# A vision layer on one core: the first picture pair in two parts ahead of the weights, its steps in another order, and the last four steps as straight code

## What is computed

```python
gray = einsum('bchw,c->bhw', x, (0.2989, 0.587, 0.114))
h = abs(conv3x3(gray, scharr)).sum(over the 2 filters) / 2
n = layernorm(h);  prev = n shifted by one row
k, v, r = (n * m_i + prev * (1 - m_i)) @ W_i.T       # m_i, W_i for i in k, v, r
wkv = recurrence over the rows (w, u, k, v)           # numerator / denominator
h = h + (sigmoid(r) * wkv) @ Wo.T
n2 = layernorm(h);  e = argmax(h_hat @ Wg.T)          # one expert for each row
h = h + gelu((n2 * scale_e + bias_e) @ W1_e + b1_e) @ W2_e + b2_e
```

## Time and profile before

| | us |
|---|---|
| median of 3 runs | 1120.14 (1119.8 to 1122.0) |
| the profiled execution | 1121.44 |
| its span, first to last instruction | 1119.8 |
| TensorE busy in the span | 1069.8 (96%) |
| VectorE busy | 1024.5 (91%) |
| ScalarE busy | 989.4 (88%) |

### The profile page before, as it was taken

The page is one execution under the profiler, slowest core; times in us unless marked ns, Lnnn a source line. Parts: engine busy times, 40 slices in busy tenths (PEclk is TensorE's granted clock), DMA queues, the critical chain, the costliest instruction groups (busy, mean ns, idle before and its releaser), DMA issues.

```text
span 1119.8 us, 17777 instructions
## 1 busy us (share of the span) xinstructions
PE 1069.8 (96%) x6097; PEld 777.9 (69%) x6097; DVE 1024.5 (91%) x1867; ACT 989.4 (88%) x1581; POOL 283.0 (25%) x298
## 2 busy tenths in 40 slices
PE   7767999999999999999999999999999999999887
PEld 2344777777777777778777777777777777777665
DVE  4689999999999999999999999999999999999820
ACT  0569899999999999999999999999999999999642
POOL 3431123322212333322122332231223332210001
PEclk8889999999999999999999999999999999999989
DMA  9697878999889889999999899999999899771223
GB/s 172 148 177 152 161 108 159 168 179 188 171 150 163 162 158 175 174 189 171 152 162 169 161 158 181 182 173 156 161 166 163 157 179 181 125 120 27 37 38 38
DMA packets 177776, 168.31 MB, mean 150 GB/s; under 512 B 14352, under 2 KB 177742, under 8 KB 177742
## 3 DMA queue, kind: packets, MB, share of 16 engines
q1 hardware_dynamic: 126358, 118.50, 48.3%
q0 software_dynamic: 50048, 48.25, 34.0%
q10 hardware_dynamic: 1336, 1.12, 0.5%
HBM read 102.80 MB, written 80.76 MB: 164 GB/s over the span
## 4 chain that ended last, share of the span: by engine, by line
PE 87%; ACT 5%; DVE 3%; SPq 2%; issue 1%; POOL 1%; DMA 0%; POOLq 0%; DVEq 0%; ACTq 0%
PE bank L1628 24%; PE bank L1803 20%; PE bank L1742 15%; PE bank L1727 10%; PE bank L1666 9%; PE bank L1637 5%; PE bank L1649 1%; PE bank L1804 1%; PE bank L1757 1%; PE bank L1767 1%; SPq L336 1%; ACT hidden L1278 1%; SPq L361 1%; DMA planes<-in_x_dram 0%; DVE gap L590 0%
## 5 line engine op out<-in xcount | busy, mean ns | idle before, releaser
L1803 PE MATMUL bank<-w_sb,hidden 128*128 128x256 f32 x1024 | 240.8, 382 | 3.7 <-ACT hidden L1278 3.6
L475 POOL DMA_DIRECT2D out_dram<-moe x64 | 76.3, 1192 | 619.7 <-ACT moe L1290 600.2
L1803 PEld LDWEIGHTS bank<-w_sb,hidden 128*128 128x128 f32 x1024 | 185.6, 191 | 33.2 <-ACT hidden L1278 5.2
L1727 PE MATMUL bank<-w_o_t,den 128*128 128x256 f32 x512 | 120.8, 390 | 4.1 <-DVE den L663 4.1
L1666 PE MATMUL bank<-rows_in,conv_w 102*32 102x512 f32 x960 | 110.3, 599 | 0.0
L1742 PE MATMUL bank<-normed_hi,w_hi 128*128 128x512 f32 x256 | 110.0, 430 | 0.0
L1727 PEld LDWEIGHTS bank<-w_o_t,den 128*128 128x128 f32 x512 | 97.0, 194 | 17.7 <-DVE den L663 5.3
L1742 PE MATMUL bank<-normed_lo,w_hi 128*128 128x512 f32 x256 | 101.0, 394 | 0.0
L1742 PE MATMUL bank<-normed_hi,w_lo 128*128 128x512 f32 x256 | 100.9, 394 | 0.0
L605 DVE TENSOR_TENSOR_SCAN max_state<-neg_exp_w,bank 128x256 f32<-128x256 f32 x128 | 80.7, 672 | 12.3 <-PE bank L1628 12.3
L590 DVE SCALAR_TENSOR_TENSOR mixed_vr<-normed,params,normed_t 128x512 f32<-128x512 f32 x128 | 91.3, 755 | 0.0
(11 more groups left out here) (166 smaller groups left out, 2679.1 us busy)
## 6 DMA issues: line engine op xcount, KB each, us to landing
rows_in<-gray_dram SPq DMA_DIRECT2D x180, 256.0 KB
planes<-in_x_dram SPq DMA_DIRECT2D x120, 256.0 KB, 8.1
gray_dram<-planes POOLq DMA_DIRECT2D x120, 256.0 KB, 5.8
out_dram<-resid SPq DMA_DIRECT2D x64, 256.0 KB, 4.7
out_dram<-moe POOLq DMA_DIRECT2D x64, 256.0 KB, 5.3
gray_dram<-in_x_dram SPq DMA_DIRECT2D x60, 256.0 KB, 4.9
rows_in<-gray_dram SPq DMA_DIRECT2D x120, 24.0 KB
rows_in<-in_x_dram SPq DMA_DIRECT2D x9, 256.0 KB
```

The lines of the kernel that those rows point to most:

```text
L475: pool.dma_start(out_rows(at.j, at.u - FFN, half), moe[:, 2 * half:2 * half + 2, :], accum_op=ALU.add).then_inc(added[half], 16)
L1727: ins = pe.matmul(bank[BANK_WO[half]][:, i * D:(i + 1) * D], rwkv[:, 2 * kt + i, half * P:(half + 1) * P], w_t[3][:, kt, :], start=(kt == ...
L1803: pe.matmul(ps, hidden[:, m, i, rows], w2_sb[:, m, :], start=(m == 0), stop=False)
```

## The change

Four things are changed together; the loop is left as it is.

1. The first pair is loaded by `load_first_colors` in two halves of the rows (`s_top_rows`, then `rows_loaded[0]`), 20 DMAs instead of 10. SyncE then waits until the whole pair has landed before it issues `Wk`, `Wv`, `Wr` and all that follows. `scharr_dj` is made on VectorE instead of loaded by five DMAs, ahead of the colour weights, which take three wide products instead of six; `b2` comes by ScalarE's queue. Eight warm-up matmuls instead of 14.
2. ScalarE writes the high part of a weight straight from the bank (`high_weights`), VectorE the low part (`low_weights`); GpSimd splits nothing.
3. `first_steps` stands in a new order on VectorE, ScalarE and TensorE.
4. `run_steps` ends after step 32; steps 33 to 36 are straight code, `last_steps()`, on VectorE, ScalarE and TensorE, in an order of their own. SyncE and GpSimd keep the `step` function there.

```diff
-WARM_UP = 7
+WARM_UP = 4
+LAST_STEPS = 1
...
+        def load_first_colors(eng, i):
+            base = i * NCOL * T * D
+            for half, loaded in ((0, s_top_rows), (1, rows_loaded[0])):
+                tile = half * TILES // 2
+                for color in range(NCOL):
...
+                    eng.dma_start(rows_in[0][ROW_TILE * color:ROW_TILE * (color + 1), tile:tile + TILES // 2, i, :], src
+                                  ).then_inc(loaded, 16)
...
-            load_colors(sp, 0, 0)
-            for src, dst in zip((Wk, Wv), w_raw):
+            load_first_colors(sp, 0)
+            sp.wait_ge(rows_loaded[0], 16 * X_DMAS)
+            for src, dst in zip((Wk, Wv, Wr), w_raw):
                 sp.dma_start(dst, src.rearrange("(a p) c -> p a c", p=P)).then_inc(s_w_in, 16)
...
-            pool.wait_ge(s_act_setup, 5)
-            split_weights(0)
-            split_weights(1)
-            split_weights(2)
             run_steps(pool, step)
...
+            def low_weights(i):
+                done(dve.tensor_tensor(w_lo[i][:, :, :].rearrange("p a d -> p (a d)"), bank[BANK_W[i]][:, :],
+                                       w_hi[i][:, :, :].rearrange("p a d -> p (a d)").bitcast(F32), ALU.subtract))
...
+            def high_weights(i):
+                act.activation(w_hi[i][:, :, :].rearrange("p a d -> p (a d)"), bank[BANK_W[i]][:, :], ACT.Copy
+                               ).then_inc(s_act_setup, 1)
...
-            run_steps(pe, step, first=FIRST_STEPS)
+            run_steps(pe, step, first=FIRST_STEPS, last=LAST_STEPS)
+
+            def last_steps():
...
+                first_layer(2, FFN, pair(29, FFN), waits=False)
+                pe.wait_ge(s_result[1], 29)
+                pe.wait_ge(s_rwkv, 31)
+                output_projection(1, PROJ, pair(30, PROJ), waits=False)
```

More of the change, by code:

```diff
@@ L308, in pair, with run_steps @@
             return Step((p + stage) // UNROLL, (p + stage) % UNROLL, PAIRS)
-        def run_steps(eng, step, first=0, before={}):
+        def run_steps(eng, step, first=0, last=FFN, before={}):
             for n in range(first, 2 * UNROLL):
@@ L318, in run_steps @@
                     step(Step(j, i, PAIRS))
-            for i in range(FFN):
+            for i in range(last):
                 step(Step(PAIRS // UNROLL, i, PAIRS))
@@ L545, in _ @@
             assert own[0] == SETUP_FIRST
-            dve.wait_ge(s_scharr_dj_in, 80)
-            done(dve.tensor_scalar(scharr_dj[0:TAPS, :], scharr_dj[0:TAPS, :], 0.5 * GRAY_WEIGHTS[2], None, ALU.mult))
+            for b in range(1, 2):
+                clear_outside(b)
             for di in range(3):
@@ L1497, in first_steps @@
-                copy_v(1, WKV, pair(1, WKV), waits=False)
                 bonus_of(WKV, pair(1, WKV), waits=False)
@@ new lines, in first_steps @@
+                absolute(0, EDGE, pair(3, EDGE), waits=False)
+                absolute(1, EDGE, pair(3, EDGE), waits=False)
+                copy_normed2_high(1, PROJ, pair(0, PROJ), waits=False)
+                act.preload_act_table_set("natural_log_exp_and_others")
+                log_denominator(PROJ, pair(1, PROJ), waits=False)
+                absolute(3, EDGE, pair(3, EDGE), waits=False)
+                act.wait_ge(s_log_den, 2)
+                reciprocal(PROJ, pair(1, PROJ), waits=False)
@@ L1548, in first_steps @@
[L1548 removed]
+                act.wait_ge(s_shift[0], 4)
+                normalise(EDGE, pair(3, EDGE), waits=False)
                 act.wait_ge(s_moments[1], 2)
```

975 lines of the change are left out of this document (674 added, 301 removed).

## The result

| | us |
|---|---|
| changed kernel, median of 5 runs | 1108.02 (1101.69 to 1108.26) |
| kernel before, the 5 runs beside it | 1121.94 (1119.80 to 1122.66) |
| ratio, 95% interval | 0.987 [0.9855, 0.9885] |
| the recorded execution, and its span | 1101.69, 1100.1 |

The kernel is 13.9 us faster. The recorded execution is the shortest of the five, so its gain (19.7 us against the recorded 1121.44) is not the median's; a second recording of the same kernel stands in the first experiment.

What follows compares the result with a forecast made beforehand. TensorE bounds the middle, VectorE most of the start; the tail loses time to TensorE's waits and slow matmuls. Start 5 and tail 9 off the profiled 1121.44 give 1107.4, so 1106 for the median; range 1100 to 1113.

Steps and rivals of the forecast that it cites:

- The prediction's 8.8 us: Tail: waits for the route and output projections 30 and 31, with two slow stretches, go: 1.54 + 1.40 + 2.70 + 1.74 + 1.46.
- they stay, with one slow stretch: Tail: the second layer's waits for the last gelus (2.24 and 1.36) remain, with one slow stretch of 1.8 us.
- Rival C: Tail keeps its slow stretches, each remaining wait costing itself and up to 1.7 us: 1110; chance 0.18.
- Rival E: Start: the weights never held the picture; only the tail and the freed GpSimd (2.0) count: 1109; chance 0.07.
- A: Start: the picture pair lands later than taken, so the start gives nothing: 1111; chance 0.2.
- D: Slower: SyncE's wait holds its whole queue, costing more than start and tail give; 1123 at a release at 30; chance 0.03.
- 11.1: Start: when VectorE's colour weights are done and the first convolution starts, 5.4 us earlier; nine small scalings counted at 1.2.
- With a shorter wait ahead of it the clock may rise sooner: First convolution: a wait of 2 us for 3.78, so 12.8 to 13.55 us of convolution.
- the shorter warm-up lies under the first convolution: 0: Start: eight warm-up matmuls instead of 14 cost nothing, counted as 0.
- From there to the gray rows: Start: pair 2's rows land near 74.1, its convolution 10.6 us earlier; net 5.0 to 7.8 by TensorE, limiting the start to 5.
- B: Start gives all of VectorE's 9.5 us, planes and gray rows coming earlier than thought: 1101.5; chance 0.12.
- GpSimd's share: Start: weight splitting off GpSimd gives VectorE's mixes and residues 4.1 us back, net 2.0 us better.

Runs made afterwards that it cites:

- the first experiment: The changed kernel run again, unaltered: median 1106.16 us, its recorded execution also 1106.16.
- Experiment 3: The changed kernel with the new start kept but its last four steps by the step function as before: 1117.31 us, ratio 0.997.
- experiment 8: The changed kernel (eight warm-ups) with VectorE's nine small scalings for the gray weights moved behind the colour weights: 1103.64 us.
- experiment 5: The changed kernel with 14 warm-up matmuls, SyncE no longer waiting for the first pair's pictures before issuing the weights: 1103.81 us.
- experiment 2: The changed kernel with 14 warm-up matmuls, as before the change, instead of eight: 1102.35 us, ratio 0.9833.
- experiment 7: The changed kernel with 14 warm-up matmuls, ScalarE scaling pair 2's planes behind pair 1's fourth absolute value instead of the third: 1104.66 us.
- experiment 9: The changed kernel with 14 warm-up matmuls, GpSimd doing six unused copies and subtractions of the old splitting's size: 1106.00 us.
- experiment 11: The kernel of experiment 10 with pair 2's scalings also one place earlier on ScalarE: 1103.38 us.
- experiment 10: The changed kernel with 14 warm-up matmuls, plus seven calls of matmuls on zeros ahead of each of three TensorE waits in the start: 1102.67 us.
- experiment 6: The changed kernel with 14 warm-up matmuls, the first pair's pictures in ten whole DMAs instead of halves, SyncE's wait kept: 1108.32 us.
- experiment 4: The kernel before with only the new last four steps, nothing else of the change: 1107.94 us, ratio 0.9888.

## Why the prediction was right, and where only in the sum

1108.02 against 1106, inside 1100 to 1113, faster as forecast. But that the sum of "start 5, tail 9" came out is luck: two errors offset each other. The tail gave 13, the start as it was built 0 to 4.

**The tail: the mechanism was right, a term too small.** The prediction's 8.8 us are gone one by one: route, both output projections, their slow stretches. Gone as well are two things that it kept, 1.2 of the gelu waits (2.24 to 1.47, 1.36 to 0.93) and the slow stretch of 1.8 behind them, and all of the idle time outside the five waits (10.2 less 9.24, 1.0), of which it counted up to 0.9. The 1.3 for pair 29 did not appear. By rows: idle 10.2 less 2.4, and 5.0 of slow matmuls, make 12.8; 13.0 are measured, past the prediction's upper end of 11. The failed step is "they stay, with one slow stretch": it looked at the work ahead of a gelu and not at what had made ScalarE late, and it took the slow stretch for a fixed price of a wait. What made ScalarE late before, and the same row now:

```profile
1082.34 0.30 ACT L1258 ACTIVATE log_var<-moments,eps 128x4 f32<-128x4 f32 x1 [8.58 <-DVE moments L744]
```

```profile
1065.27 0.29 ACT L1409 ACTIVATE log_var<-moments,eps 128x4 f32<-128x4 f32 x1
```

These moments are pair 31's and hang on its output projection. Before, ScalarE waited 8.58 us for them and loaded a table (1.28 us) only then; now that projection stands ahead of the first layer, and ScalarE finds them there (the wait just before this row, 5.52 us, is for the route). Experiment 3 has the same 2.24 and 2.71 without the slow stretches behind them, 3.1 us less over the tail. Rival C fell.

**The start, the picture.** Held: the first convolution waits for VectorE's weights and not for the picture (experiment 8 moved the weights and the convolution came with them). Rival E fell with that. The picture was complete at 11.92, not at 13, and between 11.77 and 12.09 in the other recordings with halves and the wait, which ends A and D; experiment 5 shows no price of SyncE's wait beyond 1.5 us. The batching rule that the prediction set against the split (the Trainium skill, "DMA: Bandwidth & Descriptors", section "Bandwidth") is not borne out here: ten DMAs of up to 256 KB were complete 1.7 us after twenty of up to 128 KB, and the kernel with them is 6.0 us slower. Both sizes lie below the 1 MiB that the page asks for, and its figures are for DMAs issued from GpSimd, while SyncE and ScalarE issue these, several at a time.

**The start, the weights.** 11.1 was estimated; they were done at 11.56 and 12.13 in the two recordings. The mis-sized term is the nine scalings, 3.1 us for 1.2: the first three take 0.17 each as in the earlier trace rows, but the six behind them, each of which waits in the code for the one before, 0.43 each. Most of these 1.9 us did not show, since the taps came at 4.63 and not at 5.69 (1.1) and the other products took 0.4 less; that 11.1 came out so nearly is partly luck.

**The start, the clock.** Here the step failed. "With a shorter wait ahead of it the clock may rise sooner" named the right thing with the wrong size: 2 us were taken, and with eight warm-ups the wait is 3.27 to 4.24 us, about the 3.78 of before, since the warm-up now ends at 8.0 to 8.7 and the weights are late. The convolution then takes 10.48 or 12.18 us, by the execution, for 12.8 to 13.55 predicted. With 14 warm-ups the median is 4 to 6 us lower (experiment 2). The term "the shorter warm-up lies under the first convolution: 0" is the one that was wrong; its cover was not there.

**From there to the gray rows.** Predicted and read (first recording, second recording): first difference 33.9 (31.56, 33.83); GpSimd's gray 44.0 (42.95, 45.45); from there to the landing of the rows 30.06 (27.42, 27.53); rows 74.1 (70.37, 72.98). Pair 1's picture was there by 29.6, as experiment 8 shows, not at 31 to 36: the load of `W1` was not held for 6.1. TensorE's wait was 3.9 us for 5 to 8, and a second one of 4.8 to 5.1 for pair 3's rows was not foreseen. The direction holds: VectorE was 9.9 and 7.6 us ahead at the first difference, and step 6 came only 6.6 and 2.2 us earlier. The mechanism holds in part. Experiment 8 shows a lead of 2.6 us gone at pair 2's rows. But experiment 7 shows a delay of 3.5 us at pair 2's rows gone at pair 3's, so in that recording the wait that binds is one pair further on than the prediction looked. And behind pair 3's transposes the clock takes up to 2.9 us more in some recordings (the last table), for which the sum had no term. It makes 1.5 of the 4.4 us between the two recordings of the changed kernel, and some of the 6.6 may be this, too: in the recording of before, in another order, the same eight convolution matmuls took 1.94 us. B fell.

**GpSimd's share** was right: 1.41 for 2.67, made and undone in experiment 9. By that recording some 2.1 us of it reach pair 3's convolution; what reaches the end is not settled.

## What to carry to other kernels

When a change shortens the work ahead of a wait, look at what the wait does to the matmuls behind it; here six idle-looking warm-up matmuls lowered the median by 4 to 6 us, and a wait of 3 us was priced in some executions and free in others. Mark a point in the program that all work passes (here step 6's first convolution and step 33's) and read two recordings of one kernel at it before believing a difference of a few microseconds. Follow a delay from one such mark to the next, too: in experiment 7 the median moved by just what the theory said, but in the recording the delay had died out on the way and another loss had taken its place. A lead on one engine is worth only what the next late arrival leaves of it: follow that chain (here planes, scaling, additions, rows) to its own first cause before moving its middle.

## What the runs showed of the hardware

The first convolution's 96 matmuls and the idle time just ahead of them on TensorE, over twelve recordings (the thirteenth, experiment 11, has no idle time there and 10.48 too):

| recording | idle ahead, us | 96 matmuls, us |
|---|---|---|
| experiments 8, 7, 10, 2, 9, 5 | 0, 0.46, 0.74, 0.88, 1.37, 1.71 | 10.48 in each |
| experiment 6 | 2.83 | 13.53 |
| experiment 4 | 3.05 | 12.18 |
| changed kernel | 3.27 | 10.48 |
| kernel before | 3.78 | 13.55 |
| experiments 1, 3 | 4.19, 4.24 | 12.18 |

In 10.48 us all 96 ran at the higher of the two levels (2.4 GHz). Short waits never lost the clock here; of the longer ones most did, and one did not, though shorter ones did. What decides between them is open, and so the duration behind such a wait is a range and not a price.

A second place shows the same scatter. In the kernels with the new start, eight matmuls of pair 3's convolution and twelve of a projection follow one another behind pair 3's transposes:

| recording | pair 3's transposes, at us | the 20 matmuls, us | step 6, at us |
|---|---|---|---|
| experiment 2 | 98.84 | 4.06 | 142.11 |
| changed kernel | 99.44 | 4.07 | 142.75 |
| experiments 5, 1 | 98.78, 102.29 | 5.60, 5.61 | 143.63, 147.11 |
| experiments 11, 10, 9 | 97.05, 98.03, 101.56 | 6.57, 6.72, 6.57 | 142.94, 144.01, 147.55 |
| experiments 8, 6, 7, 3 | 99.25, 103.94, 99.17, 101.46 | 6.65, 6.81, 6.85, 6.91 | 145.36, 150.43, 145.68, 148.07 |

The mean granted clock of the 10 us from the first of the twenty on is 1.00 in the first two rows, 0.83 in the third and 0.66 to 0.72 in the others. From the end of the twenty to step 6 it is 34.34 to 34.39 us in all eleven, so what is lost here arrives in full. What decides is open here as well: the twenty were slow behind convolutions that ran throughout at the higher clock (2.78 us for 24 matmuls, experiments 7, 10, 11) and behind some that took 5.35 (experiments 3 and 9).

A DMA queue's issues can be held for long: four loads of planes took SyncE 9.81 us to issue, and taking a wait of 7 us out ahead of them moved them by 0.2 us (experiment 5).
